# Two layers of cross-attention and their MLPs on one core: projections over four PSUM banks, a later spread of probabilities, and the extra key's column written behind a tile's logits

## The reference, cut to what matters

```
h = layer_norm(x);  qh = (h @ wq + bq) per head (128 wide)
kh, vh = ctx @ wk + bk, ctx @ wv + bv;  kh, vh = concat(kh, bias_k), concat(vh, bias_v)
x = x + softmax(qh kh^T / sqrt(128)) vh @ wo + bo        # twice, with weights 1 and 2
x = x + gelu(layer_norm(x) @ w_fc1 + b) @ w_fc2 + b
...                                                      # second block: 16 heads of 32, a mask, an MLP
```

## Time and profile before

| what | value |
|---|---|
| median of 3 runs | 2390.76 us (2388.98 to 2396.07) |
| the profiled execution, time / span | 2392.78 us / 2391.0 us |
| PE, PEld busy | 91%, 84% of the span |
| DVE, ACT, POOL busy | 56%, 47%, 35% |
| mean granted TensorE clock | 0.964 of full speed |
| DMA | 293 MB, mean 123 GB/s |

### The profile page before, as it was taken

The page is one execution under the profiler, slowest core; times in us unless marked ns, Lnnn a source line. Parts: engine busy times, 40 slices in busy tenths (PEclk is TensorE's granted clock), DMA queues, the critical chain, the costliest instruction groups (busy, mean ns, idle before and its releaser), DMA issues.

```text
span 2391.0 us, 34442 instructions
## 1 busy us (share of the span) xinstructions
PE 2166.7 (91%) x11876; PEld 2011.8 (84%) x11876; DVE 1339.5 (56%) x3230; ACT 1119.7 (47%) x2520; POOL 842.3 (35%) x770
## 2 busy tenths in 40 slices
PE   6989989888898988989898898989899989888999
PEld 4878889887888988888898888889899978877899
DVE  5636457464654745555475554637544567768441
ACT  4433345444334543344444343444455576657464
POOL 4133252432426224241523415143266611122255
PEclk8999999999999999999999999999999999999899
DMA  4744434365453434536343363633344466665233
GB/s 150 183 107 109 125 97 102 85 177 134 118 122 86 121 94 119 123 101 141 98 113 93 96 145 89 150 96 99 93 133 125 125 175 183 178 171 137 83 114 118
DMA packets 231410, 293.32 MB, mean 123 GB/s; under 512 B 112456, under 2 KB 157640, under 8 KB 231240
## 3 DMA queue, kind: packets, MB, share of 16 engines
q1 hardware_dynamic: 231240, 291.14, 46.2%
HBM read 258.84 MB, written 28.95 MB: 120 GB/s over the span
## 4 chain that ended last, share of the span: by engine, by line
PE 68%; DVE 9%; DMA 9%; ACT 9%; issue 4%; SPq 1%; POOL 1%; ACTq 0%; DVEq 0%; POOLq 0%
PE bank L1019 63%; DMA ctxN_raw<-in_ctx 5%; DVE QU L1718 2%; PE bank L1125 2%; ACT mring L1425 2%; ACT QU L1425 2%; DMA k<-k_parts 2%; DVE tmp L1848 1%; DMA stage<-in_wk 1%; PE bank L1091 1%; ACT prob L1541 1%; PE bank L1294 1%; DVE ctxT L1718 1%; DVE prob L1904 1%; DVE lnb L1760 1%
## 5 line engine op out<-in xcount | busy, mean ns | idle before, releaser
L931 POOL TENSOR_TENSOR mring<-stage,mring 128x512 fp32r<-128x512 f32 x389 | 522.5, 1348 | 397.6 <-ACT mring L1425 385.7
L1019 PE MATMUL bank<-pT,ctxN 128*128 128x500 f32 (+3 forms) x2304 | 494.5, 367 | 52.1 <-DVE ctxN L1718 33.3
L1019 PE MATMUL bank<-ctxT,QU 128*125 128x362 f32 (+1 forms) x2496 | 463.5, 337 | 37.3 <-DVE bank L1803 30.8
L1019 PEld LDWEIGHTS bank<-pT,ctxN 128*128 128x128 f32 (+1 forms) x2304 | 392.5, 200 | 103.8 <-DVE ctxN L1718 37.4
L1718 DVE TENSOR_TENSOR QU<-bank,QU 128x400 fp32r<-128x400 f32 (+2 forms) x512 | 280.8, 570 | 343.1 <-ACT QU L1425 342.7
L1019 PEld LDWEIGHTS bank<-ctxT,QU 128*125 128x125 f32 (+1 forms) x2496 | 425.5, 189 | 50.4 <-issue 35.7
L976 POOL TENSOR_TENSOR ctxN<-ctxN_raw,ctxN 128x384 fp32r<-128x384 f32 x144 | 145.5, 1021 | 583.6 <-ACT ctxN L1425 583.6
L1019 PE MATMUL bank<-hT,mring 128*128 128x400 f32 x1656 | 326.9, 349 | 10.9 <-ACT hT L1425 6.4
L1425 ACT ACTIVATE QU<-bank 128x400 fp32r<-128x400 f32 (+2 forms) x512 | 243.1, 497 | 187.7 <-PE bank L1019 185.7
L1019 PEld LDWEIGHTS bank<-hT,mring 128*128 128x128 f32 x1656 | 305.0, 190 | 20.0 <-issue 7.1
L1425 ACT ACTIVATE pT<-bank 128x375 fp32r<-128x375 f32 (+2 forms) x336 | 152.2, 453 | 239.4 <-PE bank L1125 214.8
(11 more groups left out here) (110 smaller groups left out, 2737.0 us busy)
## 6 DMA issues: line engine op xcount, KB each, us to landing
ctxT<-c_parts SPq DMA_DIRECT2D x96, 724.0 KB, 5.6
ctxN_raw<-in_ctx SPq DMA_DIRECT2D x192, 192.0 KB, 4.4
k<-k_parts SPq DMA_DIRECT2D x96, 181.0 KB, 3.6
stage<-in_wq SPq DMA_DIRECT2D x64, 256.0 KB, 2.5
stage<-in_wk SPq DMA_DIRECT2D x64, 256.0 KB, 2.6
stage<-in_wv SPq DMA_DIRECT2D x64, 256.0 KB, 2.6
stage<-in_wo SPq DMA_DIRECT2D x64, 256.0 KB, 2.6
stage<-in_fa SPq DMA_DIRECT2D x64, 256.0 KB, 2.6
```

What stands on the lines that cost most here:

```text
L931: nc.gpsimd.tensor_tensor(lo, src, f32(hi), ALU.subtract).then_inc(S.w_ready, 1)
L1019: mm = pe.matmul(dst, parts_l[a], parts_r[b], start=first and k == 0, stop=last and k == len(order) - 1)
```

## The change

- Projections take four banks in turn in place of three, and wait for the output four back. `E_BANK` moves from 3 to 4; PE's first `extra_logits` of a group waits for `pt_lo`, and its first `project` waits until ACT has copied `E_BANK`.
- In a group of 6 heads after one of 5, the last `o` is moved behind the last `k`.
- `put_extra` moves from two steps ahead to behind the tile's own logits (it waits for `s_mm`), straight ahead of `maximum`. PE waits for `nm_ready` of two tiles back in place of `e_put`. `extra_add` moves ahead of the last `projected` of the group before.
- `normalise` scales the tile first, then copies the first column.
- `value_low` is done at once after a `v` that no `k` follows.
- SP: `spread_p0` of batch `b` is issued at the end of batch `b + 1`, and that of the last batch in the next group's projections, after its third job. At the last batch, `load_ctxT` is moved from the last tile to the fourth last step.

```diff
-        if s < before:
+        if s < before and (s < before - 1 or now <= before):
             items.append(("o", G - 1, s))
+    if now > before > 0:
+        items.append(("o", G - 1, before - 1))
...
-        M_BANK, N_BANK, E_BANK = 5, 0, 3
+        M_BANK, N_BANK, E_BANK = 5, 0, 4
...
-            return bank[PROJ_AT[key] % 3][:, 0:ROWS]
+            return bank[PROJ_AT[key] % 4][:, 0:ROWS]
...
+                if G == NG:
+                    spread_p0(G - 1, NB - 1)
                 for j in range(FIRST_JOB[G], FIRST_JOB[G + 1]):
                     load_jobs(j + 1 + MS + STAGE)
+                    if 0 < G < NG and j - FIRST_JOB[G] == 2:
+                        spread_p0(G - 1, NB - 1)
...
                     if i < NB * n and i % n == n - 1:
-                        load_ctxT(NB * G + i // n + 2)
-                    if i < NB * n and i % n == n - 1:
+                        if i // n < NB - 1:
+                            load_ctxT(NB * G + i // n + 2)
                         save_p0(G, i // n)
-                    if i >= 2 and i - 2 < NB * n and (i - 2) % n == n - 1:
-                        spread_p0(G, (i - 2) // n)
+                        if i // n > 0:
+                            spread_p0(G, i // n - 1)
...
+                    if i == group_steps(G) - 4:
+                        load_ctxT(NB * G + NB + 1)
...
-                if n >= 3:
-                    pe.wait_ge(S.proj_done, n - 2)
+                if n >= 4:
+                    pe.wait_ge(S.proj_done, n - 3)
...
+                if h == 0 and G:
+                    pe.wait_ge(S.pt_lo, last_tile(G - 1))
...
-                pe.wait_ge(S.e_put, n + 1)
+                if n >= 2:
+                    pe.wait_ge(S.nm_ready, n - 1)
...
+                    if G < NG - 1:
+                        pe.wait_ge(S.e_copied, G + 2)
...
-                if at < 2:
-                    dve.wait_ge(S.proj_mm, proj_after(G))
-                else:
-                    dve.wait_ge(S.nm_ready, n - 1)
+                dve.wait_ge(S.s_mm, n + 1)
...
+                nc.vector.tensor_scalar(x, x, rden[0:size, k:k + 1], None, ALU.mult).then_inc(S.p_ready, 1)
...
-                nc.vector.tensor_scalar(p0_col[0:size, at:at + 1], x[:, 0:1], rden[0:size, k:k + 1], None, ALU.mult)\
-                    .then_inc(S.p0_copied, 1)
-                dve.wait_ge(S.p0_copied, n + 1)
-                nc.vector.tensor_scalar(x, x, rden[0:size, k:k + 1], None, ALU.mult).then_inc(S.p_ready, 1)
+                dve.wait_ge(S.p_ready, n + 1)
+                nc.vector.tensor_copy(p0_col[0:size, at:at + 1], x[:, 0:1]).then_inc(S.p0_copied, 1)
...
                     if (kind, h) == ("o", heads(G - 1) - 1):
+                        if G < NG:
+                            extra_add(G)
                         for c in range(DC):
                             projected(g, c)
...
-                extra_add(G)
-                put_extra(first)
-                put_extra(first + 1)
+                if G == 0:
+                    extra_add(G)
                 for i in range(group_steps(G)):
                     if i < n:
+                        put_extra(first + i)
                         maximum(first + i)
-                    if i + 2 < n:
-                        put_extra(first + i + 2)
```

More of the change, by code:

```diff
@@ L1993, in _ @@
                         value_low(*late)
-                    late = (g, h) if kind == "v" else None
+                        late = None
+                    if kind == "v":
+                        if PROJ[G][PROJ[G].index((kind, g, h)) + 1][0] == "k":
+                            late = (g, h)
+                        else:
+                            value_low(g, h)
                     if (kind, h) == ("o", heads(G - 1) - 1):
+                        if G < NG:
+                            extra_add(G)
                         for c in range(DC):
```

## The result

The changed kernel takes 2301.2 us (median of 4 runs, 2295.3 to 2305.2) where the kernel before took 2393.4 (4 runs): ratio 0.9614, interval 0.9586 to 0.9643. That is faster, by 92 us where 139 were forecast, and 1 us outside the range. The profiled execution has a span of 2303.1 us against 2391.0, so 87.9 us less. One further run of the kernel before, beside the three-bank kernel, was in the slow state and took 6304 us where all its others took 2389 to 2404; it is left out.

What follows compares the result with a forecast made beforehand. PE, busy 91% of the span, was taken as the bound, with its matmuls, idle stretches and low clock. Gains of 48.5 + 23.5 + 5 + 31 + 6 + 25 = 139 us gave 2252 us, range 2230 to 2300.

Steps and rivals of the forecast that it cites:

- Four banks: Projections: a fourth bank removes PE's 65.5 us of fold waits, less new stalls; 48.5 us gained.
- the new stall behind the extra key's load: Weight queued behind `e_part` comes late: 1.4 us in each of 11 groups, 15 in all, bounds 0 and 35.
- Start of the logits: Group starts: PE no longer waits for the extra key's copy; 23.5 us gained, plus 5 of 7.3 in group 0.
- The copy ahead of `maximum`: DVE's copy, some 0.2 us a tile, now ahead of `maximum`: costs nothing, bounds -5 and +5 us.
- `ctxT` after `ctxN`: 5-head group ends: last chunks have the queue to themselves, so 31 of 33.3 us of `ctxN` waits go; bounds 20 and 33.
- the signs that the prediction names for being wrong: A group's first queries waiting for `mring`, or stalls of 1 us recurring at each head.
- The 6-head ends: Ends of 6-head groups: 6 of the 9.5 us of `QU` waits ahead of 300-column value sums go.
- The new waits: PE's first `extra_logits` and first `project`, and DVE's copy after its tile's logits: the added waits cost nothing.
- The clock: PE's low clock after `ctxN` stalls, at starts, in group 0 and at 6-head ends: 25 us come back.
- The context stall stays: Rival: ACT's or DVE's order, not the DMA, holds the `ctxN` chunk; 31 and 13.5 come back, 2297 us; chance 0.09.
- Weights: Rival: late weights in three `stage` slots set the pace, 1.1 us more some 50 times, 2302 us; chance 0.12.
- the late `ctxT`: Rival "Slower": moved `ctxT` collides with the next group's weights at first queries of 11 groups; 2395 us and more; chance 0.03.

Runs made afterwards that it cites:

- the three-bank kernel: Changed kernel with three projection banks in turn again (bank 3 idle), all else kept: 2371.9 us.
- The undone copy: Changed kernel with the extra key's copy two steps ahead again and PE waiting for it: 2325.9 us.
- the kernel with all saves late: Changed kernel with the first column's save and the spread issued behind the last `ctxN` chunk in every batch: 2218.2 us.
- the kernel with the save late: Changed kernel with only the last batch's save of the first column moved behind the `ctxN` chunks, spread left in place: 2239.2 us.

## Why the prediction was wrong, by its own steps

- **Four banks: the mechanism right, the size low.** 65.1 of the 65.5 us of waits went, and the new stall behind the extra key's load came as argued, 11.1 us in seven places for the 15 taken. The 2 us taken for the last `v_parts` were no new cost: PE waited 1.6 us for it in three places before, and 1.7 us after. Forecast 48.5; waits gave 54, and 16 more came from the folds' busy time, which the prediction's own 8.1 and 6.54 us for a head contain and its sum leaves out. The three-bank kernel puts the whole part at 71.
- **Start of the logits: right.** 23.5 us of waits went. Group 0 gave 3.2 for 5 (8.3 us of waits before, 5.1 now). The undone copy costs 25.
- **The copy ahead of `maximum`: right, nothing.** No wait of PE names it in the profile after.
- **`ctxT` after `ctxN`: this step failed,** where it says that "the last chunks now have the queue for themselves". SP's new order puts `save_p0` and a spread right ahead of them, and I gave the save's 2 KB no price. The rows had it: in the prediction's own words the extra key's "two DMAs of 4-byte elements" make the weight behind them land 5.7 us after its issue, and the save is of the same kind. 31 us were forecast, 3.1 came. Of the signs that the prediction names for being wrong neither appeared; "`ctxN` waits under 3 us" is the line of its list that failed. Its 172 GB/s, taken from the earlier trace rows, was a rate with the save in the queue.
- **The 6-head ends: the same fault,** with the sign turned. 6 us less were forecast of the 7.7 at the four ends; they are 12.6 now, 5.0 more. In the middle batches of these groups 1.9 us became 9.3. That chunks behind a save cause them is shown by the kernel with all saves late, where both are gone. Why they grew isn't shown. My reading is that PE arrives earlier, and that in the middle batches the spread no longer holds SP back.
- **The new waits:** 5.6 us more for the layer norm's sum from POOL or its turn behind DVE, not in the sum. PE now reaches it early. No run takes this apart.
- **The clock:** 25 us were forecast. PE's busy time fell by 21.9 in all, 16.2 of it in the folds, where the clock was not the reason; so some 6 us came back, since the stalls at the groups' ends, behind which the clock was low, stayed. In the kernel with the save late, where they go, the mean clock rises to 0.982.
- **The rivals.** "The context stall stays" was the right outcome (2297 forecast, 2301 measured), given 0.09, with the wrong cause: neither ACT's nor DVE's order held the chunk. That its number is so near is luck, since it also leaves out the folds' 16 us and the 18 of new waits. Weights did not set the pace (that rival's 1.1 us some 50 times is 55 us, where it writes 50), and the late `ctxT` did not collide with the next group's.

Waits account for 65.7 us of the 87.9 (53.9 folds, 23.5 starts, 3.2 group 0, 3.1 `ctxN`, less 12.4 and 5.6), and the fall of PE's busy time for 21.9.

## What to carry to other kernels

Price a DMA by its elements, not its bytes, and charge it to whatever is issued behind it: look in the queue's order for a transfer of 4-byte elements ahead of each one that an engine waits for, and move it behind. When one thing in a queue is named as what holds the next, look at all that stand between them. A move of the big transfer alone bought 25 us here, and the small one left in place kept 62. With a round of buffers, what counts is which output last used the slot; a fourth bank cost nothing and was worth 71 us.

## What the runs showed of the hardware that I had not expected

- A second write of 500 elements of 4 bytes (2 KB) ahead of a load on SP's queue made PE wait 4.6 us longer for that load. The same bytes in 125 elements of 16 made it wait 1.0 us longer.
- 1448 KB and 250 KB issued in the 2.4 us ahead of a 192 KB load let it land in 4.6 us, sooner than 2 KB in 4-byte elements with the 250 KB did (6.9 us). The mean rate was 304 GB/s with the large transfers ahead and 100 with the save ahead.
- Stalls of 1.3 to 1.7 us at every head left the granted clock at 1.00 in the two windows shown, and 590 to 622 us with three banks. In the changed kernel each of the 19 stalls of over 2 us from 60 to 1640 us was followed by 0.79 or less over the next 8 us. In other kernels some stalls of that length were not: of the eight starts with 2.5 us in the kernel before, three were followed by 1.00.
